# A three-sublayer decoder on one core: the last batch's gate products, the second chunk's scans and several waits are put in another order

## The reference

```python
# f1: gated linear attention with a decay, 16 heads
q, k, v = split(x @ Wqkv.T);  q, k = elu(q) + 1, elu(k) + 1
kv, ks = decay_scan(k * v), decay_scan(k)       # along the rows: s[t] = decay * s[t-1] + in[t]
out = q * kv / clip(sum_head(q * ks), 1e-6)
g = sigmoid(out @ Wgate.T + bgate)
f1 = (g * out + (1 - g) * v) @ Wout.T
# f2: r[t] = 0.9 * r[t-1] + ctx[t]**2;  f2 = x * r
# f3: quantized feed-forward, 512 -> 1536 -> 512
x = qdq16(x);  up = qdq16(x @ Wup4.T);  gate = qdq16(x @ Wgate4.T)
f3 = qdq16(qdq16(gate * sigmoid16(gate)) * up) @ Wdown4.T
```

## Time and profile before

| | us |
|---|---|
| median of 3 runs (2635.15 to 2637.47) | 2635.33 |
| the profiled execution | 2635.85 |
| its span | 2633.7 |
| busy: PE | 2533.0 (96%) |
| busy: DVE | 2019.5 (77%) |
| busy: ACT | 1355.5 (51%) |

### The profile page before, as it was taken

One profiled execution on the slowest core, in us unless ns is written; L12 is line 12 of the kernel. 1 busy time (PEld: TensorE's weight loads), 2 busy tenths in 40 slices (PEclk: granted clock), 3 DMA queues, 4 the chain that ended last, 5 costly groups with the idle time before them and its releaser, 6 DMA issues.

```text
span 2633.7 us, 31986 instructions
## 1 busy us (share of the span) xinstructions
PE 2533.0 (96%) x11190; PEld 2117.6 (80%) x11190; DVE 2019.5 (77%) x2820; ACT 1355.5 (51%) x1727; POOL 389.3 (15%) x278
## 2 busy tenths in 40 slices
PE   7999999999999997999999999999999699999998
PEld 5888888888888886888888878888888588888886
DVE  7899999999999994555555459987777766666664
ACT  4455555555565654333333358888888522222222
POOL 0000000000000000000000003322222133333331
PEclk9999999999999998999999999999999899999999
DMA  4011222121111225555555458877777635555552
GB/s 176 9 64 72 95 108 76 72 80 72 72 72 68 102 110 176 188 183 186 185 183 184 167 192 295 288 259 258 255 255 255 261 146 221 211 211 211 211 211 92
DMA packets 146282, 429.85 MB, mean 163 GB/s; under 512 B 73136, under 2 KB 81584, under 8 KB 106416
## 3 DMA queue, kind: packets, MB, share of 16 engines
q1 hardware_dynamic: 143920, 412.39, 43.2%
q10 hardware_dynamic: 2304, 16.78, 1.5%
HBM read 235.67 MB, written 177.21 MB: 157 GB/s over the span
## 4 chain that ended last, share of the span: by engine, by line
PE 57%; issue 1%; DVE 1%; DMA 1%; ACT 1%; POOL 0%; SPq 0%; POOLq 0%; DVEq 0%; ACTq 0%
PE pair L1962 13%; PE pair L1963 13%; PE pair L1964 13%; PE pair L2014 6%; PE pair L2016 6%; PE pair L2015 6%; PE pair L1972 0%; DMA ff_gs<-gate_ints 0%; DMA ff_q<-x_ints 0%; DVE ff_sr L1884 0%; DMA up_products<-ff_group 0%; ACT ff_group L1499 0%; ACT ff_group L1633 0%; DVE ff_stats L1918 0%; DVE ff_group L1915 0%
## 5 line engine op out<-in xcount | busy, mean ns | idle before, releaser
L1962 PE MATMUL pair<-ff_hi,wide_h 128*128 128x512 f32 x1536 | 600.5, 391 | 17.7 <-DVE ff_lo L1680 13.9
L1964 PE MATMUL pair<-ff_hi,wide_l 128*128 128x512 f32 x1536 | 599.2, 390 | 0.0
L1963 PE MATMUL pair<-ff_lo,wide_h 128*128 128x512 f32 x1536 | 598.9, 390 | 0.0
L1499 ACT ACTIVATE ff_group<-pair,ff_scales 128x512 f32<-128x512 f32 x384 | 257.4, 686 | 303.8 <-PE pair L1964 293.4
L1962 PEld LDWEIGHTS pair<-ff_hi,wide_h 128*128 128x128 f32 x1536 | 289.3, 188 | 78.4 <-DVE ff_lo L1680 14.3
L1964 PEld LDWEIGHTS pair<-ff_hi,wide_l 128*128 128x128 f32 x1536 | 289.1, 188 | 60.3
L1963 PEld LDWEIGHTS pair<-ff_lo,wide_h 128*128 128x128 f32 x1536 | 289.4, 188 | 59.7
L2014 PE MATMUL pair<-wide_h,ff_hi 128*128 128x512 f32 x768 | 299.6, 390 | 25.0 <-DVE ff_lo L1900 23.4
L935 PE MATMUL pair<-xh,wide_h 128*128 128x512 f32 x768 | 302.1, 393 | 12.7 <-DVE xl L575 12.7
L936 PE MATMUL pair<-xl,wide_h 128*128 128x512 f32 x768 | 300.3, 391 | 0.0
L939 PE MATMUL pair<-xh,wide_l 128*128 128x512 f32 x768 | 300.2, 391 | 0.0
(11 more groups left out here) (228 smaller groups left out, 4603.5 us busy)
## 6 DMA issues: line engine op xcount, KB each, us to landing
gate_products<-ff_group SPq DMA_DIRECT2D x48, 1024.0 KB, 4.0
ff_raw<-gate_products SPq DMA_DIRECT2D x48, 1024.0 KB, 5.7
up_products<-ff_group SPq DMA_DIRECT2D x48, 1024.0 KB, 4.3
ff_raw<-up_products SPq DMA_DIRECT2D x48, 1024.0 KB, 9.2
gate_ints<-ff_gs SPq DMA_DIRECT2D x48, 512.0 KB, 2.7
ff_gs<-gate_ints SPq DMA_DIRECT2D x48, 512.0 KB, 9.9
xt_raw<-in_xT SPq DMA_DIRECT2D x64, 256.0 KB, 3.4
csq<-in_ctx_rows SPq DMA_DIRECT2D x16, 1024.0 KB, 7.3
```

The lines of the kernel that those rows point to most:

```text
L1499: act.activation(group[:, g, m * T:(m + 1) * T], out_ps[(GM * g + m) % 6][:], ACT.Copy, scale=s_x).then_inc(evacuated, 1)
L1962: pe.matmul(o, wh[:, m, k], hi[:, par, k], start=(k == 0), stop=False)
L1963: pe.matmul(o, wh[:, m, k], lo[:, par, k], start=False, stop=False)
L1964: mm = pe.matmul(o, wl[:, m, k], hi[:, par, k], start=False, stop=(k == KC - 1))
```

## The change

In every step of the first part TensorE makes the second chunk's products before the gate tiles instead of behind them; `context_carry` stays behind the gate tiles and now follows them directly. ScalarE does the second chunk's exponentials before the gates' tanh. VectorE does both the first and the second chunk's scans before any `scale_difference`; `scale_difference` of tile 0 moves from the end of the step before to this place. At the end of the step `first_residual(s, 1)` and `reciprocals` move ahead of `split_x` and `local_sums`.

Elsewhere: the first step's first product, and the second part's first tile, wait for one piece of the inner dimension at a time instead of four; unread matmuls, whose results nobody uses, are more in step 0 (14 to 20 and 6 to 20) and new at the start of the second part (8); the transposing DMA of the second up batch is issued before the first up step instead of behind a wait for GpSimd; and the last batch's sum, norm and store are done for each of its four groups of 128 rows by itself.

```diff
@@ -423,14 +423,8 @@
                         weights_high(KC)
-                    if back:
-                        gate_tanh(s, 0)
-                    if due:
-                        squares(1, s - 1, (0, 1))
-                    if back:
-                        gate_tanh(s, 1)
                     if due:
-                        squares(1, s - 1, (2, 3))
-                    if back:
-                        gate_tanh(s, 2)
-                    if back:
-                        gate_tanh(s, 3)
+                        squares(1, s - 1, range(TT))
+                    if front:
+                        front_tile(s, 1, par)
+                        if not back:
+                            weights_high(KC + 1)
                     if due:
@@ -439,2 +433,4 @@
                         for m in range(KC):
+                            gate_tanh(s, m)
+                        for m in range(KC):
                             act.wait_ge(mixed, KC * (s - 1) + m + 1)
@@ -442,5 +438,2 @@
                     if front:
-                        front_tile(s, 1, par)
-                        if not back:
-                            weights_high(KC + 1)
                         front_tile(s, 2, par)
@@ -723,4 +716,2 @@
                         piece_scaled(piece - 1)
-                    if back:
-                        scale_difference(s, 1)
                     if due:
@@ -732,3 +723,11 @@
                         norm_bias(1, s - 1)
+                    if front:
+                        if not back:
+                            weights_low(KC)
+                        front_scans(s, 1, par)
+                        if not back:
+                            weights_low(KC + 1)
                     if back:
+                        scale_difference(s, 0)
+                        scale_difference(s, 1)
                         add_v(s, 0, par)
@@ -748,8 +747,3 @@
                         front_product(s, 0)
-                        if not back:
-                            weights_low(KC)
-                        front_scans(s, 1, par)
                         front_product(s, 1)
-                        if not back:
-                            weights_low(KC + 1)
                     if back:
@@ -769,8 +763,2 @@
                         front_product(s, 3)
-                    if nxt:
-                        split_x(s + 1, (0, 1))
-                    if front:
-                        local_sums(s + 1, 1 - par)
-                    if piece is not None and 0 <= piece < NPIECE:
-                        piece_rounded(piece)
                     if back:
@@ -779,4 +767,10 @@
                         reciprocals(s)
+                    if nxt:
+                        split_x(s + 1, (0, 1))
+                    if front:
+                        local_sums(s + 1, 1 - par)
                     if back:
                         first_residual(s, 2)
+                    if piece is not None and 0 <= piece < NPIECE:
+                        piece_rounded(piece)
                     if nxt:
@@ -801,4 +795,2 @@
                         piece_scales(piece + 1)
-                    if front:
-                        scale_difference(s + 1, 0)
 
@@ -843,2 +835,3 @@
                 def last_step():
+                    scale_difference(NB, 0)
                     turned_low(range(0, 4))
@@ -928,7 +921,7 @@
             def _(pe):
-                def product(out, stat, mov, between=None):
-
-
+                def product(out, stat, mov, between=None, ahead=None):
                     n = len(stat)
                     for k in range(n):
+                        if ahead:
+                            ahead(k)
                         (sh, sl_), (mh, ml) = stat[k], mov[k]
@@ -953,6 +946,5 @@
                         pe.wait_ge(wal_ready, c + 1)
-                    if c == 0:
+                    first = isinstance(b, int) and n == 0
+                    if c == 0 and not first:
                         pe.wait_ge(xl_ready, KC * (b + 1))
-
-
                     wait(pe, phi_ready, n - 1)
@@ -960,3 +952,4 @@
                         wait(pe, o_ready, KC * b)
-                    product(qk_ps[c % 2][:, 0], w_tile(0, c), x_halves)
+                    product(qk_ps[c % 2][:, 0], w_tile(0, c), x_halves,
+                            ahead=(lambda k: pe.wait_ge(xl_ready, k + 1)) if first else None)
                     product(qk_ps[c % 2][:, 1], w_tile(1, c), x_halves).then_inc(qk_ready, 1)
...
@@ -1041,2 +1034,4 @@
                         turn_weights(range(0, 6))
+                    if front:
+                        qkv(s, 1)
                     if back:
@@ -1045,4 +1040,2 @@
                         turn_weights(range(6, 12))
-                    if front:
-                        qkv(s, 1)
                     if back:
@@ -1063,5 +1056,5 @@
                         pe.wait_ge(const_dve, 8)
-                        unread(14)
+                        unread(20)
                         denominators(s)
-                        unread(6)
+                        unread(20)
                         turn_reciprocals(s)
@@ -1273,3 +1266,3 @@
 
-                def up_step(b, par, ahead):
+                def up_step(b, par, ahead, turns=True):
                     for g in range(NG):
@@ -1281,3 +1274,3 @@
                             load_gate(b + 1, g)
-                            if g == 0:
+                            if g == 0 and turns:
                                 turn(b + 1, 1 - par)
@@ -1313,4 +1306,7 @@
                 for g in range(NG):
+                    if g == NG - 1:
+                        turn_free(NB + 1, 1, 16 * (NB // 2))
                     load_gate(0, g)
-                up_step(0, 0, True)
+                turn(1, 1)
+                up_step(0, 0, True, turns=False)
                 load_weights(6)
...
@@ -1466,3 +1462,5 @@
                 root(NB - 2)
-                root(NB - 1)
+                for j in range(TT):
+                    pool.wait_ge(ve_ready, NB + j)
+                    pool.tensor_tensor(rstd[:, j:j + 1], var_eps[:, j:j + 1], mhalf[:, j:j + 1], ALU.pow).then_inc(rstd_ready, 1)
 
...
@@ -1667,3 +1665,9 @@
                 normalise(NB - 2, 0)
-                normalise(NB - 1, 1)
+                for j in range(TT):
+                    cols = slice(j * HID, (j + 1) * HID)
+                    act.wait_ge(nmr_ready, NB + j)
+                    act.activation(x2_res[:, 1, cols], x2_res[:, 1, cols], ACT.Identity, scale=rstd[:, j:j + 1],
+                                   bias=nmr[:, j:j + 1]).then_inc(norm_ready, 1)
+                    act.wait_ge(norm_ready, TT * (NB - 1) + j + 1)
+                    act.dma_start(out[NB - 1][:, j], x2_res[:, 1, cols]).then_inc(d_stored[1], 16)
 
@@ -1922,2 +1926,27 @@
 
+                def last_bias(j):
+                    row = slice(j, j + 1)
+                    dve.wait_ge(rstd_ready, NB + j)
+                    dve.scalar_tensor_tensor(nmr[:, row], msum[:, row], -0.5, rstd[:, row], ALU.mult, ALU.mult).then_inc(nmr_ready, 1)
+
+                def last_sums():
+
+                    dve.wait_ge(d_x2_in[1], 16 * (NB // 2))
+                    for j in range(TT):
+                        n = TT * (NB - 1) + j + 1
+                        cols, row = slice(j * HID, (j + 1) * HID), slice(j, j + 1)
+                        dve.wait_ge(part_used, TT * (NG * NB - 1) + j + 1)
+                        dve.scalar_tensor_tensor(x2_res[:, 1, cols], banks[TT + j][:], s_o, x2_res[:, 1, cols],
+                                                 ALU.mult, ALU.add).then_inc(sum_ready, 1)
+                        if j > 0:
+                            last_bias(j - 1)
+                        dve.wait_ge(sum_ready, n)
+                        dve.bn_stats(stats[:, j], x2_res[:, 1, cols]).then_inc(stats_ready, 1)
+                        if j == 0:
+                            dve.wait_ge(norm_ready, TT * (NB - 1))
+                        dve.wait_ge(stats_ready, n)
+                        row_moments(dve, stats[:, row], msum[:, row], mdiff[:, row], msq[:, row], var_eps[:, row],
+                                    moments_ready, square_ready, ve_ready, NB + j)
+                    last_bias(TT - 1)
+
                 def norm_bias(b):
@@ -1951,4 +1980,3 @@
                 norm_bias(NB - 2)
-                sums(NB - 1, 1, NB // 2 - 1)
-                norm_bias(NB - 1)
+                last_sums()
 
@@ -1960,2 +1988,4 @@
                     for k in range(KC):
+                        if first and m == 0:
+                            pe.wait_ge(lo_ready, k + 1)
                         o = out_ps[m % 6][:]
@@ -1975,3 +2005,4 @@
                 def step(s, par, weights=None, first=False, new=None):
-                    pe.wait_ge(lo_ready, KC * (s + 1))
+                    if not first:
+                        pe.wait_ge(lo_ready, KC * (s + 1))
                     for m in range(MT):
@@ -1985,2 +2016,8 @@
                         turn(new, (2, 3))
```

(24 more changed lines are left out.)

2 lines of the change are left out of this document (1 added, 1 removed).

## The result

| | before | after |
|---|---|---|
| median, us | 2635.72 (2635.15 to 2637.47, 4 runs) | 2684.20 (2680.97 to 2684.84, 4 runs) |
| ratio | | 1.0183, 95% interval 1.0171 to 1.0195 |
| span of the profiled execution | 2633.7 | 2682.9 |

What follows compares the result with a forecast made beforehand. VectorE's queue, 58.36 us a step, plus its waits was taken to bound the first part's steps, TensorE the second part. Steps +50.4, step 1 +2.5, clock +4 and ends -14.6 made +42.3 on 2635.33: about 2678 us, range 2652 to 2704.

Steps and rivals of the forecast that it cites:

- start and step 0: First product starts sooner and unread matmuls save some half-clock time; -1.5 us, between +1 and -3.3.
- step 1: TensorE sets the pace, gaining waits before carry and broadcast and losing the old 1.4 us; +2.5 us, between 0 and 4.
- steps 2 to 15: Each first-part step takes 63.0 us, 3.6 more than 59.40; 14 of them cost 50 us.
- the clock: TensorE's new waits in the steps may bring half clock, 1.7 us a time; 4 us in all, between 0 and 24.
- second part's start: Tile 0 starts 2.8 us sooner and eight unread matmuls take half-clock time; -4.2 us, between -2.8 and -5.1.
- up products: Earlier transpose ends ScalarE's wait for integers, TensorE's 3.8 us wait and the half clock after; -5.5 us, between -3 and -5.5.
- end: One norm instruction instead of four behind the last sum, and a quarter-size last store; -3.4 us, between -2.4 and -3.6.
- rival of TensorE as the bound: VectorE has time to spare, so TensorE's 1.43 us wait is simply gone in the steps; 2601 us, faster; 6%.
- (a): VectorE's wait for ScalarE's four squares before the variance: 0.4 us left of 0.74; its 0.30 us tanh wait goes.
- (b): At the gate, VectorE stands still 3.35 us a step for tanh, about 1.9 and 1.4 at scale_difference 2 and 3.
- (c): Behind the gate, TensorE waits 1.7 us at the carry, and VectorE 0.9 us at phi of the fourth chunk.
- (d): End of step: TensorE's 1.43 us wait goes, some 2 us before the broadcast comes, hidden at gate tile 2; VectorE 0.

Runs made afterwards that it cites:

- extra_dve: Four unused 256-column VectorE multiplications a step ahead of the first chunk's add_v, added to ends_only; 2647.52 us, 1.0044 of the kernel before.
- end_order: ends_only plus the changed kernel's end of step: second residual and reciprocals ahead of split and local sums; 2637.51 us, 1.0009 of the kernel before.
- fill: Changed kernel with VectorE's `largest` moved between scale_difference 1 and 2, where it waits for tanh; 2685.57 us, 1.0188 of the kernel before.
- carry_late: Changed kernel with context_carry behind the third chunk's products, VectorE's carried sums behind its scans, front_product 0 sooner; 2668.64 us, 1.0117 of the kernel before.
- steps_only: Kernel before with only the first part's steps in the new order; 2695.72 us, 1.0229 of the kernel before.
- ends_only: Changed kernel with the first part's steps put back in the order of before, all other edits kept; 2622.91 us, 0.9950 of the kernel before.
- ends_late: ends_only with two 1 MB down-weight loads moved from ahead of the third up batch's transpose to behind later up steps; 2619.07 us, 0.9932 of before.
- ends_no8: ends_only without the eight unread matmuls at the second part's start; 2623.35 us, 0.9951 of the kernel before.

## Why the prediction was right

The sum by its own steps, in us; what was measured is read from the start times of the broadcasts, of matmuls in the gate, up and down products, and of the last instructions in the two timelines:

| step | predicted | measured |
|---|---|---|
| start and step 0 | -1.5 | -0.8 |
| step 1 | +2.5 | +0.4 |
| steps 2 to 15, the clock in them | +50.4, +4 | +57.4, +3.2 |
| second part's start | -4.2 | -3.7 |
| up products | -5.5 | -3.3 |
| down products | 0 | -0.4 |
| end | -3.4 | -3.6 |
| sum | +42.3 | +49.2 |

Little of the hit is owed to errors that cancel: the steps alone were 7.0 us over the forecast, step 1 2.1 us under it.

- **What bounds.** For the order before, extra_dve shows that it is VectorE's queue: added work counts in full. The rival of TensorE as the bound falls with the result (2684 us for its 2601) and with end_order, where its wait for xrow went and the steps without a fall stayed at 59.2 to 59.4 us. For the new order, fill and carry_late show that the step is set by a way through both engines, from gate tile 2 over tanh, VectorE and the carry to phi of the fourth chunk. The table of five orders shows that VectorE's queue without its waits keeps its 58.36 us within 0.16 us. By itself it doesn't say which engine bounds: the same sum can be made for TensorE (58.15 + 5.30 us in the changed kernel).
- **(a)** 0.47 us for 0.4. **(b)** 2.00 + 1.30 us for 1.9 + 1.4. The 0.05 us of each hand-over in its sum stand in no row; the sum of 3.35 came out as 3.30. **(c)** the carry 1.57 us for 1.7, phi of the fourth chunk 1.02 for 0.9. **(d)** the broadcast 1.59 us for 2, hidden by gate tile 2.
- **What the step's sum missed**: 63.45 came for 63.0. The terms above are 0.14 us low in all, 0.17 is a wait for the second output tile that I had not listed, and 0.14 is in no wait. Each is small, and 14 steps make 6.3 us of them. Nor were the 14 steps alike: step 15 was 57.86 us before and 61.82 after.
- **The clock** cost 3.2 us for 4, for the reason given: behind the broadcast a fall is hidden, behind gate tile 2 it counts. How many falls would come behind gate tile 2 followed from nothing, and that 4 us were near is luck: two came here, one in steps_only, two in fill.
- **Step 1.** The new order costs 2.4 us there (61.49 us against 59.06 in ends_only), for the 2.5 predicted (the terms given there, 1.7 + 2 - 1.4, make 2.3). But the 10.24 us at half clock of the earlier trace rows reached 4.4 us into step 1 of before, whose 61.08 us are 2.0 more than those of ends_only. With the fall this went too; I had booked its going to step 0.
- **The up products** were mis-sized by 2.2 us. I held that the third chunk's integers would be covered by six banks. The third batch's transpose, behind two loads of 1 MB, held TensorE for 2.1 us instead. So the first wait's going gave 5.7 us, as forecast, and the next one took 2.4 back; ends_late removes it.
- **(b) and (c) added up** in the prediction as if they were two losses. They add, but fill shows that they are one delay of TensorE's chain that VectorE meets at two places: filling the first brought nothing, because the second grew by as much.

The Trainium skill, "Perfetto Trace Analysis", section "Identifying the Most-Contended Engine", says to optimize the engine with the highest occupancy first, but to judge TensorE by its share of peak rate and by the busy share of its weight loads, and not by that of its matmuls. By matmuls TensorE stood ahead here (57.98 us for 57.59 of VectorE); by weight loads it is 49.38 of 59.40 us, 83%, for VectorE's 97%, and VectorE is the engine to serve. The trace agrees: the change took TensorE's 1.43 us away and lengthened the step by 4.05 us, and in end_order, which did only that, the steps without a fall gained 0.2 us at most.

## What to carry to other kernels

Where two engines of a step are within a few per cent of each other, add up each one's queue without its waits: the step is the longer queue plus the waits that fall into it. A wait that goes from the other engine is worth only what it takes off those waits: nothing for the 1.43 us at xrow, 1.00 us a step for the 1.57 at the carry. Ahead of a move, ask what stood between an instruction and its buffer's release, since a long piece of work there (here 8.16 us of products between gate and carry, and a chunk of scans between two gate tiles) is a cover that goes with it. Work put into a wait helps only if the waited-for chain doesn't depend on that engine again before the step ends.

## What the chip showed that was not expected

- Waits of TensorE for xrow of up to 1.43 us in 14 steps, before and in ends_only, were followed by no fall of the clock. The same wait, 1.6 to 1.95 us long in 13 steps of extra_dve, was followed by ten falls of 3.41 us, from 2.4 to 1.2 GHz. Waits at the broadcast, 1.59 us but for a first one of 2.02, were followed by 11 falls in 15 in end_order; eight unread matmuls in them took 12.3 us off.
- The length of the wait alone does not decide. In the changed kernel 1.57 us at the carry were followed by a fall in none of 15 steps, 2.0 to 2.5 us at gate tile 2 in two of eight, and 1.6 to 1.7 at the broadcast in six of 15. What decides between them no run shows.
- The same fall costs 0.8 to 2.0 us or nothing. It costs nothing where TensorE's next long wait hangs on what VectorE did earlier, as at gate tile 2.
- The third batch's transposing DMA takes 8.0 us in ends_late, and 9.3 to 10.3 in the kernels with two loads of 1 MB ahead of it (the kernel before, the changed one, ends_only and ends_no8).
